# First layer's edges of a four-layer graph network: row buffers' scatter waited for by halves, next group's new sources counted ahead of the attribute projections

## The reference, cut to what matters

```
h    = relu(layernorm(x)) @ w_in + b_in                         # once per node, before this stage
Wij  = (softplus(f_ij @ w_f1 + b_f1) - log 2) @ w_f2 + b_f2     # per edge
Wij  = Wij * rcut_ij[:, None]
x_ij = h[idx_j] * Wij                                           # per edge; summed by idx_i in the next stage
...
ek, ev = edges @ Wek, edges @ Wev                               # third layer's projections of the 128 edge attributes
```

## Time and profile before

| | us |
|---|---|
| three runs | 7666.76, 7705.08, 7707.18 |
| median | 7705.08 |
| span of the profiled execution | 7688.3 |
| this stage, first to last burst's first scatter | 488.1 to 2225.8 |

### The profile page before, as it was taken

One profiled execution on the slowest core, in us unless ns is written; L12 is line 12 of the kernel. 1 busy time (PEld: TensorE's weight loads), 2 busy tenths in 40 slices (PEclk: granted clock), 3 DMA queues, 4 the chain that ended last, 5 costly groups with the idle time before them and its releaser, 6 DMA issues. The chain is left out here.

```text
span 7688.3 us, 103954 instructions
## 1 busy us (share of the span) xinstructions
PE 3918.9 (51%) x22797; PEld 3082.2 (40%) x22798; DVE 3809.0 (50%) x8547; ACT 1438.4 (19%) x3669; POOL 3692.0 (48%) x3791
## 2 busy tenths in 40 slices
PE   6746666556769523333343334333246635555556
PEld 4534445444546322222241222222135534444555
DVE  7845555555669633333353434333488833333333
ACT  6623333333320200000010000000023310101101
POOL 0054445444531166666616666666324345556552
PEclk9867777777789755555565555555569955555556
DMA  2066656656644211111116777776744411111111
GB/s 86 7 187 184 183 179 189 185 178 188 196 122 102 49 45 45 44 46 45 45 37 221 237 227 233 220 225 218 152 112 133 115 51 43 44 44 45 44 45 37
DMA packets 906173, 920.69 MB, mean 120 GB/s; under 512 B 329848, under 2 KB 744650, under 8 KB 905994
## 3 DMA queue, kind: packets, MB, share of 16 engines
q1 hardware_dynamic: 754906, 542.66, 25.6%
q0 software_dynamic: 138544, 371.96, 15.9%
q10 hardware_dynamic: 12672, 5.51, 0.3%
HBM read 678.28 MB, written 241.47 MB: 120 GB/s over the span
## 5 line engine op out<-in xcount | busy, mean ns | idle before, releaser
L953 POOL DMA_INDIRECT by_src<-edges_rows,edges_pos x832 | 860.0, 1034 | 903.9 <-issue 681.5
L1502 POOL DMA_INDIRECT edges_kv<-kv,edges_idx x896 | 915.3, 1021 | 700.5 <-issue 492.9
L2068 POOL DMA_INDIRECT sum_rows<-table,sum_idx x832 | 823.0, 989 | 649.9 <-DVE sum_msg L2112 311.1
L1258 POOL DMA_INDIRECT sum_rows<-table,sum_idx x832 | 787.2, 946 | 552.0 <-issue 246.4
L1335 PE MATMUL sum_p_sum<-sum_hot,sum_rows 128*128 128x128 f32 x1664 | 396.2, 422 | 830.4 <-DVE a_acc L1314 576.2
L1335 PEld LDWEIGHTS sum_p_sum<-sum_hot,sum_rows 128*128 128x128 f32 x1664 | 350.6, 312 | 876.2 <-DVE a_acc L1314 626.5
L2167 PE MATMUL sum_p_sum<-sum_hot,sum_msg 128*128 128x128 f32 x1664 | 425.2, 399 | 528.2 <-issue 459.2
L726 PE MATMUL edges_p_attr<-k_wekv,edges_attr 128*128 128x256 f32 x1664 | 575.9, 506 | 47.8 <-issue 30.9
L2167 PEld LDWEIGHTS sum_p_sum<-sum_hot,sum_msg 128*128 128x128 f32 x1664 | 359.8, 297 | 595.9 <-issue 594.4
L1612 PE MATMUL edges_p_q<-q_q,edges_src_hotT 128*128 x2688 | 418.1, 284 | 348.6 <-issue 282.7
L2127 DVE TENSOR_TENSOR a_acc<-a_acc,sum_p_sum 128x128 f32 x832 | 239.8, 288 | 694.1 <-DMA edges_attr<-in_attr128T 556.3
(11 more groups left out here) (376 smaller groups left out, 7648.6 us busy)
## 6 DMA issues: line engine op xcount, KB each, us to landing
edges_ekv<-by_src SPq DMA_DIRECT2D x112, 1024.0 KB
v<-edges_kv SPq DMA_DIRECT2D x112, 512.0 KB
sum_vv<-v SPq DMA_DIRECT2D x112, 512.0 KB, 3.9
edges_attr<-in_attr128T SPq DMA_DIRECT2D x104, 512.0 KB
edges_near<-h_in SPq DMA_DIRECT2D x832, 48.0 KB
sum_rows<-by_src SPq DMA_DIRECT2D x112, 264.0 KB, 3.0
edges_src_b<-rel SPq DMA_DIRECT2D x112, 256.0 KB
edges_dst_b<-dst SPq DMA_DIRECT2D x104, 256.0 KB
```

The lines of the kernel that those rows point to most:

```text
L953: nc.gpsimd.indirect_dma_start(Dr.by_src0, bass.IndirectOffsetOnAxis(pos[:, q, j:j + 1], 0), rows[:, q % 2, j, :], None).then_inc(scattere ...
L1258: nc.gpsimd.indirect_dma_start(rows[:, q, j, :], None, Dr.table, bass.IndirectOffsetOnAxis(idx[:, q, j:j + 1], 0)).then_inc(fetched[q], 16)
L1502: nc.gpsimd.indirect_dma_start(kv[:, q, j, :], None, Dr.kv, bass.IndirectOffsetOnAxis(idx[:, q, j:j + 1], 0)).then_inc(fetched[q], 16)
L2068: nc.gpsimd.indirect_dma_start(rows[:, q, j, :], None, Dr.table, bass.IndirectOffsetOnAxis(idx[:, q, j:j + 1], 0)).then_inc(fetched[q], 16)
```

## The change

Two edits, and the waits that follow from them.

1. `scattered` becomes four semaphores instead of two: for each half of the `rows` buffer one for tiles 0 to 3 and one for tiles 4 to 7. ScalarE waits for the first of them ahead of chunk 0 and for the second ahead of chunk 2, instead of for all eight scatters ahead of chunk 0. VectorE's `positions` waits for both. VectorE's `products` now waits for all four copies of its group (`attr_kept` at 4g+6) instead of the first only.
2. On TensorE, `sources(g + 1, ...)` is issued after `p_first` and ahead of `attributes(g, q, 0)`, instead of after `attributes(g, q, 1)`.

```
-    scattered = K.soft[0:2]
-    K.soft_count = [NG // 2 * G * 16] * 2 + [0] * 2
+    scattered = [K.soft[0:2], K.soft[2:4]]
+    K.soft_count = [NG // 2 * (G // 2) * 16] * 4
...
                 mm.then_inc(first_ready, 1)
+                if not last:
+                    sources(g + 1, 1 - h)
                 attributes(g, q, 0)
                 targets(g, q, near_loads)
                 attributes(g, q, 1)
-                if not last:
-                    sources(g + 1, 1 - h)
                 pe.wait_ge(sp_ready, g + 2)
...
-                if uses is not None:
-                    act.wait_ge(scattered[h], uses * 16 * G)
-                    act.sem_inc(tick, 1)
                 for c in range(4):
+                    if uses is not None and c % 2 == 0:
+                        act.wait_ge(scattered[h][c // 2], uses * 16 * (G // 2))
+                        act.sem_inc(tick, 1)
                     act.wait_ge(attr_ps, 4 * g + c + 1)
...
                 if uses is not None:
-                    dve.wait_ge(scattered[h], uses * 16 * G)
-                    dve.sem_inc(tick, 1)
+                    for half in range(2):
+                        dve.wait_ge(scattered[h][half], uses * 16 * (G // 2))
+                        dve.sem_inc(tick, 1)
...
                 dve.wait_ge(hd_ready, g + 3)
-                dve.wait_ge(attr_kept, 4 * g + 3)
+                dve.wait_ge(attr_kept, 4 * g + 6)
...
-                        nc.gpsimd.indirect_dma_start(Dr.by_src0, bass.IndirectOffsetOnAxis(pos[:, q, j:j + 1], 0), rows[:, q % 2, j, :], None).then_inc(scattered[q % 2], 16)
+                        nc.gpsimd.indirect_dma_start(Dr.by_src0, bass.IndirectOffsetOnAxis(pos[:, q, j:j + 1], 0), rows[:, q % 2, j, :], None).then_inc(scattered[q % 2][j // (G // 2)], 16)
             for h in range(2):
-                pool.wait_ge(scattered[h], NG // 2 * G * 16)
+                for half in range(2):
+                    pool.wait_ge(scattered[h][half], NG // 2 * (G // 2) * 16)
```

## The result

The changed kernel takes 7524.6 us (median of 4 runs, 7495.4 to 7540.6) where before takes 7706.1 (4 runs, 7666.8 to 7710.4) on the same chip: a ratio of 0.9765, 95% interval 0.9731 to 0.9798. The profiled execution spans 7494.1 us, 194.2 less than before's.

The account below looks back on a forecast made before the run. Late TensorE semaphores during GpSimd's indirect DMA bursts were taken to bound the edge stage. 7688.3 - 104 = 7584 us, other terms 0; adding half of the profiled execution's 17 us below the median gave 7590, range 7440 to 7725.

Parts of the forecast that it names:

- The late semaphore of L718 bounds the stage: First layer's edge stage: TensorE's semaphores reach waiters late during bursts, L862 7.6 us late; moving L718 takes places off the path.
- In nearly all rounds: Sign in the changed kernel's timeline: L862 starts within 0.3 us of L900's end in nearly all rounds.
- C: nothing: Rival: L862 is late wherever L718 stands, or something else holds VectorE; 7688 to 7705 us; chance 0.13.
- At 15.58 they save 87 x 1.20 = 104 us.: Edge stage: 87 ordinary intervals shorten from 16.78 to 15.58 us, L806 still 11.9 us after the burst's start.
- rival A: Filter's semaphore moves up too, L763 directly following the projections: rounds of 13.99 us, saving 243 us, 7445 us; chance 0.20.
- the eight pairs of before: Edge stage: eight times two bursts back to back, then a long interval; 278 us together, taken as unchanged by the edit.
- Rival B: Bursts go back to back, delaying TensorE's releases: rounds of 17.4 us, 7743 us, slower by 0.7%; chance 0.20, partly mixed near 7690.
- Halves at 0: ScalarE's first copy may start after half of group g-2's scatters land: 0 to 4 us gained, taken as 0.
- The products' later wait at 0: VectorE's products wait for all four copies: last copy ends 7.9 us into the burst, L910 starts at 13.9 or later; nothing.
- VectorE's work in the burst: VectorE beside GpSimd's scatters: 0 or 8 x 1.09 us a round, taken as 0, hidden by 5.2 us of GpSimd idle.
- the other rule weighed: TensorE semaphores: some 26 ns per increment whatever else goes on, so new_ready was never late and moving it gives nothing.
- The added waits at about 0.1 us each: One on VectorE, one on ScalarE per group: cost nothing on an idle engine, 21 us if no cover were left.

Follow-up runs that it names:

- the gate: Changed kernel, GpSimd also waiting before each burst but the last for the second of the next group's four attribute projections: 0.9658 and 0.9663 against before.

## Why the prediction was right, and where it was not

**The late semaphore of L718 bounds the stage.** Right on kind A. With L718 ahead of the burst, L862 starts 0.08 us after L901 (forecast: within 0.3), its waits fall from 492 to 42.5 us (forecast: under 100), and the move with the products' later wait has the whole gain (0.9747) while halves have none (1.0035). "In nearly all rounds" was too much: L862 starts within 0.3 us of L901's end in 70 of 103 rounds and within 0.5 in 89, where before it was 1 and 3. "C: nothing" is excluded. On kind B the semaphore is prompt, and the same edit gives 1.1% through another chain.

**"At 15.58 they save 87 x 1.20 = 104 us."** This term was mis-sized. The stage gave back 200 us, and its mean round is 14.92 us where the forecast's sign was 15.6 to 15.9. The step behind it took L806 to stay 11.9 us after the burst's start, because it did so in the earlier trace rows and in the earlier trace rows; it came at 9.07 in the round shown, and at a median 9.1 in the ordinary ones. The difference of 2.86 us is the whole distance from 15.58 to 12.70, since the other terms (1.97 and 1.66) held. The earlier trace rows both had L718 inside the burst, so they could not show what its absence does to the filter's release. The earlier trace rows could, and rival A was built on them; its 13.99 us was nearer to the ordinary rounds' 13.3 than the forecast was. I gave A 0.20 because it rested on one round. The sum also kept the eight pairs of before (278 us) as they were; there are 20 long rounds now.

**Rival B came with it.** B was to decide once L806 starts earlier than about 8 us into the burst. It starts at 9.1 in the round shown, and earlier than 8 us in only 10 of the 83 ordinary rounds, and still the gap between bursts is only 1.8 us (553.58 to 555.41). In 25 of 103 rounds it fell to 1.2 or less, and in 20 of these a round of 21.5 us followed. Two mechanisms of the rivals thus ran together, A in most rounds and B in a fifth: 83 x 13.3 + 20 x 21.5 = 1534 us, the stage's 1537 within rounding. Without the long ones the stage would take 20 x (21.5 - 13.3) = 164 us less. That the result lies near 7590 is partly the meeting of these two, and not the forecast's own sum.

That a short gap causes the long round was not tested: the gate ran on kind B alone. What speaks for it is the count (20 of 25 short gaps, none of the wider ones), and that four of the five exceptions had a pause inside the burst instead. On kind B before has 51 gaps under 1.3 us and no round of 18 us or more. So the long round was seen only where releases are late.

**Halves at 0.** Right on kind A by the run of halves alone (1.0035). The row that it was read from, 4.2 us of waits for the DMAs, was weak evidence: that trace has 4354 recorded steps of the two scatter semaphores in the stage, of the 13312 that 832 scatters of 16 steps make, so a wait for a DMA can stand in it as one for something else. Wrong on kind B, where that wait is 382 us and the halves give 3.4%. No row of the trace before could say so, and the trace was of one chip.

**The products' later wait at 0.** No two runs on one chip differ in it alone; 0.9747 and 0.9765 both have it. The traces bear the 0 out: on kind A the last copy of a group ends 2.6 us or more ahead of the products in all 104 groups of before, 2.9 or more in the change and 1.8 or more in the move without halves, and `w_cut`, for which the products wait as well, is finished after it each time.

**VectorE's work in the burst.** In the round shown the eight scatters take 10.87 us (542.71 to 553.58), where the earlier trace rows had 10.40; three of them last 1.38, 1.35 and 1.23 us instead of 0.96. The 1.38 is no work of the change, since the second scatter of the round in the earlier trace rows took 1.38 too (at 1292.04). The other two, fifth and sixth of the burst, are: over 1 us in 80 and 68 of 104 bursts, in before in 8 and 9. A median burst went from 10.23 to 10.86 us. That is in the direction of the Trainium skill, SBUF — State Buffer, section "SBUF: two separate sides", and within the 0.2 to 1 us that was estimated; no view says in which mode the VectorE instructions beside them run. It was to be hidden by 5.2 us of idle time; with rounds of 12.7 us only 1.8 are left, so it does take part in closing the gap. On the other rule weighed, in the Trainium skill, TensorE: Matmul & The Clock Gate, section "The cost: per-tile semaphore tail", kind B agrees in size inside a burst as well (0.04 us from L718's end to L862), and kind A does not. The page fits its figure to a series of matmul tiles and has no term for what other engines do; "whatever else goes on" was the prediction's reading of it.

**The added waits at about 0.1 us each.** No run here shows this price; the sum took it as 0.

## What to carry to other kernels

When a wait is released late, moving its producer out of the bad stretch can help more than its own wait shows: on kind A the release behind it came 2.8 us earlier as well. A row taken with the old order in place can't bound that; look for a round in the trace that already has the new form, even if there is only one. When a chain of such waits gets short, ask what the gap was good for before counting its removal as gain. And a stage of waits may be bound by different waits on two chips: an edit that is worth nothing on one (halves, 1.0035) can be the larger part on the other (0.9662), so take the trace from the kind that the kernel will run on, and keep edits that are free on either. A wait that a trace doesn't name is no proof of no wait, where the trace lacks records.

## What the runs showed of the hardware

- Chips of two kinds run the same program at 7702 to 7706 and at 6618 to 6622 us. In the stage looked at, the difference is 1737.7 against 1395.9 us for the 103 rounds. While GpSimd issues indirect DMAs, the waiting engine starts 6.5 and 7.6 us after TensorE's last matmul in the rounds shown of kind A and 0.25 and 0.04 us after it in those of kind B; the semaphore's recorded step is late by a median 5.9 us on A and by 0.015 us at most on B (`w_ready`, before). The issue of a scatter does not differ: a median one takes 960 ns on A and 961 ns on B in the changed kernel.
- What makes a chip one or the other stays open. Two more things differ in the traces. On A matmuls with no wait between them start up to 3.5 us apart (0.08 us at most on B). And A's traces lack records: before's has 36,968 steps of semaphores by DMAs in the whole execution, B's has 93,893 for the same program. The record has a profiled span for every execution, so no run here tells whether the lateness would be there without the recording.
- On kind A, 20 of 25 gaps of 1.2 us or less between two bursts are followed by a round of 18.6 to 22.7 us, in most of which TensorE issues matmuls one by one with 1.2 us of idle time between them. That the gap is the cause was not tested.
- Scatters with a fifth of the bytes change the rounds by nothing on kind B (11.21 against 11.17 us). Of each burst, tiles 0 to 3 land 1.7 us earlier and tiles 4 to 7 0.4 us.
